# One coefficient multiplication of 528 elements in place of two of 264 on GpSimd, in a graph-attention loop

## What is computed

```python
seq = (x @ W_seq).reshape(N, H, DH)
score1 = jnp.einsum('nhd,d->hn', seq, a1)
score2 = jnp.einsum('nhd,d->hn', seq, a2)
scores = score1[:, :, None] + score2[:, None, :]
scores = jax.nn.leaky_relu(scores, negative_slope=ALPHA)
scores = scores + (1.0 - adj)[None, :, :] * MASK_VAL
attn = jax.nn.softmax(scores, axis=-1)
hidden = jnp.einsum('hij,jhd->ihd', attn, seq).reshape(N, D_IN)
hidden = hidden @ W_out + b_out
return jax.nn.elu(hidden)
```

## Time and profile before

| | |
|---|---|
| median of 3 runs | 1006.75 us (1005.38 to 1009.63) |
| the profiled execution | 1007.81 us, of which the span of the trace is 1006.0 us |
| PE busy | 969.1 us, 96% of the span |
| DVE busy | 773.8 us, 77% |
| ACT busy | 699.7 us, 70% |
| POOL busy | 361.0 us, 36% |
| the L1011 multiplications | 64, 150.8 us together, mean 2375 ns |
| granted TensorE clock, mean | 0.996 |

### The profile page before, as it was taken

One profiled execution on the slowest core, in us unless ns is written; L12 is line 12 of the kernel. 1 busy time (PEld: TensorE's weight loads), 2 busy tenths in 40 slices (PEclk: granted clock), 3 DMA queues, 4 the chain that ended last, 5 costly groups with the idle time before them and its releaser, 6 DMA issues.

```text
span 1006.0 us, 27591 instructions
## 1 busy us (share of the span) xinstructions
PE 969.1 (96%) x11402; PEld 747.0 (74%) x11402; DVE 773.8 (77%) x1110; ACT 699.7 (70%) x1065; POOL 361.0 (36%) x314
## 2 busy tenths in 40 slices
PE   7998999999999999999997999999999999999998
PEld 6877999999999999998774555544444469974554
DVE  6798999999999999965898544558786666546564
ACT  4479999999999999985776444444455566656441
POOL 3112466676677677743552000000185000016500
PEclk9999999999999999999999999999999999999999
DMA  9941111111111111390795000020063134462342
GB/s 247 107 75 44 64 45 45 44 65 45 44 44 44 45 60 50 104 348 12 250 311 185 2 1 1 1 85 1 32 215 129 44 108 130 132 193 84 95 132 104
DMA packets 55889, 94.74 MB, mean 94 GB/s; under 512 B 6016, under 2 KB 30208, under 8 KB 55264
## 3 DMA queue, kind: packets, MB, share of 16 engines
q1 hardware_dynamic: 40352, 66.87, 20.0%
q0 software_dynamic: 7296, 12.59, 7.0%
q10 hardware_dynamic: 8128, 13.60, 4.0%
HBM read 79.54 MB, written 26.08 MB: 105 GB/s over the span
## 4 chain that ended last, share of the span: by engine, by line
PE 41%; DVE 5%; DMA 4%; issue 1%; ACT 1%; SPq 0%; POOL 0%; DVEq 0%
PE bank L1939 16%; PE bank L1468 15%; DMA xr<-in_x 2%; PE bank L2016 2%; DMA xs<-sorted_latent_rows 2%; DVE hid L1249 1%; PE bank L1969 1%; DVE hid L1246 1%; PE bank L1924 1%; DVE stat L1251 1%; PE bank L1922 1%; PE bank L1960 1%; PE bank L1966 1%; PE bank L1967 1%; PE bank L1986 1%
## 5 line engine op out<-in xcount | busy, mean ns | idle before, releaser
L797 ACT ACTIVATE arena<-arena 128x1024 fp8e4<-128x1024 f32 x320 | 336.9, 1135 | 2.6 <-ACT arena L789 1.8
L1068 PE MATMUL bank<-arena 128*128 128x132 f16 x4096 | 285.0, 221 | 8.3 <-DVE arena L913 6.9
L1068 PEld LDWEIGHTS bank<-arena 128*128 128x128 fp8e4 x4096 | 245.0, 97 | 10.5 <-DVE arena L913 8.3
L1011 POOL TENSOR_TENSOR arena<-arena 128x264 f32<-128x264 f32 x64 | 150.8, 2375 | 102.3 <-DVE arena L884 83.7
L1468 PE MATMUL bank<-xt,up_parts 128*128 128x512 f16 x768 | 176.2, 379 | 2.2 <-DVE up_parts L1452 2.2
L1939 PE MATMUL bank<-down_parts,h_parts 128*128 128x512 f16 x768 | 176.0, 379 | 0.1
L1072 PE MATMUL bank<-arena 128*128 128x66 f16 x4096 | 172.8, 196 | 0.0
L884 DVE TENSOR_SCALAR arena<-arena 128x1024 uint8<-128x1024 f32 x192 | 156.7, 884 | 0.0
L1072 PEld LDWEIGHTS bank<-arena 128*128 128x128 fp8e4 x4096 | 153.9, 98 | 0.0
L1939 PEld LDWEIGHTS bank<-down_parts,h_parts 128*128 128x128 f16 x768 | 74.3, 98 | 90.9 <-issue 2.1
L1468 PEld LDWEIGHTS bank<-xt,up_parts 128*128 128x128 f16 x768 | 74.8, 98 | 87.0 <-issue 2.9
(11 more groups left out here) (277 smaller groups left out, 1406.4 us busy)
## 6 DMA issues: line engine op xcount, KB each, us to landing
arena<-s_rows SPq DMA_DIRECT2D x32, 512.0 KB, 3.5
sorted_latent_rows<-zeros ACTq DMA_DIRECT2D x1, 4992.0 KB, 22.7
xs<-sorted_latent_rows SPq DMA_DIRECT2D x39, 128.0 KB, 2.2
sorted_expert_rows<-expert_y SPq DMA_DIRECT2D x39, 128.0 KB, 1.7
arena<-in_adjT POOLq DMA_DIRECT2D x8, 512.0 KB, 27.7
up_rows_sb<-in_up_rows SPq DMA_DIRECT2D x4, 1024.0 KB, 10.4
xr<-in_x SPq DMA_DIRECT2D x16, 256.0 KB, 5.0
down_sb<-in_downT ACTq DMA_DIRECT2D x4, 1024.0 KB, 9.6
```

The source lines that it names most:

```text
L797: last = nc.scalar.activation(m8[:, k, j, :], s1b[:, k % 2, :], ACT.Sigmoid, bias=bias_now[:, k % 2, j:j + 1], scale=STEEP, saturate=False)
L1011: last = nc.gpsimd.tensor_tensor(scaled[:, k % 2, :, c * W1:(c + 1) * W1], sums[:, k % 2, :, c * W1:(c + 1) * W1], coef[:, h, tiles, c:c + ...
L1068: last = nc.tensor.matmul(o, m8[:, k, j, i * P:(i + 1) * P], vs[:, b, j, :], start=(j == 0), stop=(j == T - 1))
```

## The change

The loop over the two halves is gone. One instruction multiplies the 8 tiles x 2 halves x 33 columns of a unit, 528 elements a partition, with the coefficient broadcast over the 33 columns. Its result signals `scaled_step` as the second of the two did. The addition behind it, all waits and all other engines' instructions are as before.

```diff
                     h = 2 * p + k % 2
                     tiles = slice((k // 2) * IT, (k // 2 + 1) * IT)
                     pool.wait_ge(sums_ready, 4 * p + k + 3)
-                    for c in range(2):
-                        last = nc.gpsimd.tensor_tensor(
-                            scaled[:, k % 2, :, c * W1:(c + 1) * W1], sums[:, k % 2, :, c * W1:(c + 1) * W1],
-                            coef[:, h, tiles, c:c + 1].to_broadcast([P, IT, W1]), ALU.mult)
-                    last.then_inc(scaled_step, 1)
+                    nc.gpsimd.tensor_tensor(
+                        scaled[:, k % 2, :, :].rearrange("p t (c w) -> p t c w", c=2),
+                        sums[:, k % 2, :, :].rearrange("p t (c w) -> p t c w", c=2),
+                        coef[:, h, tiles, :].rearrange("p t (c o) -> p t c o", o=1).to_broadcast([P, IT, 2, W1]),
+                        ALU.mult).then_inc(scaled_step, 1)
                     pool.wait_ge(scaled_step, 4 * p + k + 1)
                     nc.gpsimd.tensor_tensor(hid[:, tiles, h, :], scaled[:, k % 2, :, 0:W1],
                                             scaled[:, k % 2, :, W1:], ALU.add).then_inc(sums_free, 1)
```

## The result

The changed kernel takes 1014.49 us (median of 5 runs, 1011.02 to 1016.04), the kernel before 1007.63 us in 5 runs beside it. The ratio is 1.0067, with a 95% interval of 1.0049 to 1.0085: slower by 6.8 us of 1007.6 (4.9 to 8.6). A second measurement on another occasion gave 1.0068 (1.0045 to 1.0091). Forecast were +6.7 us and 1013.5.

A forecast was written before the change was run, and what follows sets the result against it. DVE was taken to set the pace of the attention loop, by a small lead over PE. Terms 10.8 - 3.9 - 0.2 = +6.7 us, on 1006.75, gave 1013.5 us; range 1007.5 to 1018.5.

The forecast's parts named there:

- DVE sets the pace: Attention loop: DVE needs 46.60 us a pair of heads, PE 46.25 of its own; PE waits 0.34 us.
- The longer multiplication in the gap: POOL's multiplication between L892 and L899, 528 elements for 264, holds DVE 0.40 us longer, 27 times: +10.8 us.
- The give-back: At k = 0, POOL's first L1001 starts earlier and delays DVE's compares less: 0.65 us back, six times, -3.9 us.
- The end: After the last unit POOL alone holds up the barrier; one multiplication takes 1.06 us against 1.24 for two: -0.2 us.
- nothing is given back: Rival: L1001 meets the k = 0 compares as before, +10.6 us, 1017.4; chance 0.20, shared with a longer hold.
- The other side: Rival: hold between L892 and L899 doesn't grow, or DVE goes first; 1002.4 at the least, near 1004; chance 0.10.

The follow-up runs named there:

- run 3: Changed kernel, with the first product of POOL's loop body held back until DVE's collect (L906) has ended; 1018.86 us, ratio 1.0127 to the kernel before.
- run 4: Changed kernel, POOL released after L892, addition a unit later: 1008.41 us, ratio 0.9987; a second kernel, released when the compares end, addition in the gap: 1008.16 us, 0.9988.
- run 2: Kernel before, its two multiplications re-split into 132 then 396 elements (1004.58 us, ratio 0.9976), and in a second kernel 396 then 132 (1013.04 us).
- the first kernel of run 4: Changed kernel, with POOL released when L892 ends, the addition made a unit later and DVE's collect waiting for the multiplication; 1008.41 us, ratio 0.9987.

## Why the prediction was right

**DVE sets the pace**: right. The waits of PE grew to 1.39 (1.4 forecast), stand 47.64 us apart (47.6 forecast), and run 3 shows the next microsecond on DVE coming out as well. The lead was small, as stated, but 0.5 us a pair and not 0.34: PE's own pair was put at 46.25 and is 46.08 in run 4, where DVE falls under PE and the gain stops. This moves no term of the sum, since the change made DVE longer.

**The longer multiplication in the gap**: the mechanism is right, the size was a little low. The growth was put at 0.40 us and is 0.43 (3.264 to 3.696), so the term is 27 x 0.432 = 11.7 us and not 10.8. The slope of 1.53 ns came from two sizes read on different instructions of DVE, 264 on L899 and 512 on a compare. With run 2 there are four sizes on L899, and they give 1.66 ns. By the 2.6 cycles an element of the GPSIMD Engine Reference (the Trainium skill; section 3, Performance versus the Vector engine) the growth would have been 0.57, as an estimate. The rows give less, for the hold and for the instruction itself: alone, behind the last unit, the merged multiplication takes 1.08 us, where one of 264 takes 0.62, so 264 elements more take 0.46 us; and one of 528 holds DVE for 0.88.

```profile
474.35 1.08 POOL L1010 TENSOR_TENSOR arena<-arena 128x528 f32<-128x528 f32 x1 [5.91 <-DVE arena L906]
```

**The give-back**: right, 0.68 us six times for the 0.65 stated, 4.1 us. It was the term least supported by rows, and run 3 confirms it by itself.

**The end**: the multiplication alone takes 1.08 us in place of 1.24, so 0.2 us as stated. The sum of the measured terms is 11.7 - 4.1 - 0.2 = 7.4 us; the attention ends 7.3 us later; the median moved by 6.8 (4.9 to 8.6). The 6.7 forecast is within these; that it lies within 0.1 of the median is luck, since the terms as measured add up to 0.7 more.

**The rivals.** That nothing is given back was put at +10.6 us, and run 3 is that case: 1.27% or 12.8 us, of which the trace of its attention shows 383.3 - 371.6 = 11.7. The other side needed DVE to go first between L892 and L899; POOL won that moment again 27 times of 27. The 4.2 us of PE's waits that I had given that rival to win were never reached: run 4, which has no hindered L899 at all, still begins the unit at 124.89, and ends the attention 1.6 us earlier. The rule of the SBUF page of the Trainium skill (SBUF — State Buffer, Who interferes with whom) is that the one who issues first holds the shared ports for the whole instruction. These rows agree with it as to the order: POOL had asked inside L892, ahead of L899. The hold, 0.88 us for 528 elements, is shorter than the 1.08 us that the instruction takes alone.

## What to carry to other kernels

When GpSimd and VectorE run side by side on SBUF operands, a GpSimd instruction can cost little by its own duration and much by the elements it has when it is let in between two VectorE instructions, here 1.66 ns for each: read it as the lengthening of the VectorE instruction behind it. Merging instructions saves a start on GpSimd and makes exactly this piece longer; where VectorE sets the pace, a short piece ahead, or a release that comes once VectorE's long instruction runs, beside one that reads PSUM, is worth more than fewer instructions. And before such a gain is chased, ask how far the next engine is: here it was 0.5 us a pair.

## What the runs showed that I had not expected

PE's idle time with no semaphore behind it, 0.2 to 0.8 us at a time between 428 and 463 us, grew from 0.5 us (0.8 in the second trace) to 1.8 us in the very version in which DVE had not held PE up since 125 us. It took a good part of that version's gain. No run was made on its cause, but the traces point at PE's own instructions. In all ten, each of these 19 idles ends 2.2 to 2.6 us after a packet of 16 KB starts on the DMA queue that carries instructions. Those packets start 5.7 to 6.0 us apart on average in the loop, and the ones ahead of the idles come 6.1 to 7.0 us after the one before, where the weights of the next stage are being loaded:

```profile
400.00:420.00 20.00, 20.00 (x449) 20.00 (x446) 19.93 (x19) 19.33 (x20) 11.35 (x8) 1.00 0.33 113
...
432.00:438.00 6.00, 5.17 (x119) 5.04 (x117) 4.05 (x5) 5.10 (x17) 4.24 (x2) 1.00 1.04 359
```

These are two windows of the first kernel of run 4: the DMA engines are busy for 0.33 of the one and all of the other, in which the longest idle lies. That the loads delay the instructions is an argument from these times and is not shown.
